# Attention output of two pairs of heads formed together in one full PSUM bank

## What is computed

```python
q = (xn @ Wq).reshape(b, n, h, dh).transpose(0, 2, 1, 3)      # 16 heads of 64
k, v = jnp.split(x @ Wkv, 2, axis=-1)                          # and two null keys and values for each head
q = _l2norm(q) * q_scale
k = _l2norm(k) * k_scale
sim = jnp.einsum('bhid,bhjd->bhij', q, k) * SCALE + slopes * bias   # causal, 258 keys
attn = jax.nn.softmax(sim, axis=-1)
out = jnp.einsum('bhij,bhjd->bhid', attn, v)
return out.transpose(0, 2, 1, 3).reshape(b, n, h * dh) @ Wout
```

## Time and profile before

| | |
|---|---|
| median of 3 runs | 492.96 us (492.75 to 495.38) |
| the profiled execution's own time | 497.05 us |
| its span, first to last instruction | 495.3 us |
| mean granted clock of TensorE | 0.956 of full speed |
| busy: TensorE, VectorE, ScalarE, GpSimd | 427.6, 372.1, 357.9, 322.0 us |

### The profile page before, as it was taken

One profiled execution on the slowest core, in us unless ns is written; L12 is line 12 of the kernel. 1 busy time (PEld: TensorE's weight loads), 2 busy tenths in 40 slices (PEclk: granted clock), 3 DMA queues, 4 the chain that ended last, 5 costly groups with the idle time before them and its releaser, 6 DMA issues.

```text
span 495.3 us, 10749 instructions
## 1 busy us (share of the span) xinstructions
PE 427.6 (86%) x2809; PEld 307.0 (62%) x2809; DVE 372.1 (75%) x1419; ACT 357.9 (72%) x1098; POOL 322.0 (65%) x492
## 2 busy tenths in 40 slices
PE   4846715999997998999999999999899999989985
PEld 3735413777775766767676666667566666767663
DVE  5698412656653996898799789889888988988884
ACT  3354512666666977988897897899789789878864
POOL 3748779700003789698877968877796897787150
PEclk9959765999999999999999999999999999999999
DMA  8961111222220000000001000000100000010010
GB/s 240 319 217 38 52 50 48 66 80 77 81 66 21 2 13 11 3 23 21 3 1 40 6 1 24 21 3 2 44 1 1 23 23 2 1 43 2 2 44 11
DMA packets 29739, 21.37 MB, mean 43 GB/s; under 512 B 3528, under 2 KB 27376, under 8 KB 29552
## 3 DMA queue, kind: packets, MB, share of 16 engines
q1 hardware_dynamic: 26816, 16.46, 11.2%
q0 software_dynamic: 2048, 4.20, 2.8%
q10 hardware_dynamic: 816, 0.03, 0.1%
HBM read 12.41 MB, written 8.26 MB: 42 GB/s over the span
## 4 chain that ended last, share of the span: by engine, by line
PE 34%; DVE 22%; POOL 18%; issue 11%; ACT 8%; another core or an unknown queue 4%; ACTq 1%; DMA 1%; DVEq 0%; POOLq 0%
PE bank L970 5%; POOL rnorm L425 5%; POOL arena_b L505 4%; DVE arena_b L899 4%; PE bank L972 4%; PE bank L1189 4%; PE bank L971 4%; PE bank L1119 4%; DVE arena_b L914 3%; DVE arena_b L876 3%; PE bank L1110 3%; POOL arena_b L441 2%; POOL rpow L428 2%; DVE probT L924 2%
## 5 line engine op out<-in xcount | busy, mean ns | idle before, releaser
L675 ACT ACTIVATE arena_b<-arena_b,nmx 128x130 f32<-128x130 f32 (+1 forms) x256 | 115.0, 458 | 30.6 <-DVE nmx L899 19.9
L899 DVE CUSTOM_DVE_ANT_0 arena_b<-bank,bias 128x130 f32<-128x130 f32 (+1 forms) x256 | 81.2, 355 | 24.0 <-PE bank L1119 19.0
L914 DVE TENSOR_SCALAR arena_b<-arena_b,rden 128x130 f32<-128x130 f32 (+1 forms) x256 | 82.6, 370 | 4.5
L428 POOL TENSOR_TENSOR rpow<-ssm,mhalf 128x8 f32<-128x8 f32 x32 | 53.0, 1655 | 34.1 <-DVE ssm L887 33.4
L1110 PE MATMUL bank<-ident,arena_b 128*128 128x128 f32 x384 | 67.0, 283 | 5.7 <-DVE arena_b L914 5.6
L441 POOL TENSOR_TENSOR arena_b<-arena_b,rnorm 128x512 f32<-128x512 f32 x64 | 68.1, 1065 | 5.0
L1119 PE MATMUL bank<-arena_a 64*128 64x130 f32 (+1 forms) x512 | 59.5, 351 | 0.8 <-ACT arena_a L636 0.8
L1110 PEld LDWEIGHTS bank<-ident,arena_b 128*128 128x128 f32 x384 | 43.8, 141 | 24.8 <-DVE arena_b L914 13.6
L883 DVE TENSOR_REDUCE ssq<-arena_b 128x8 f32<-128x512 f32 x64 | 43.6, 682 | 14.0 <-issue 13.3
L613 ACT ACTIVATE arena_b<-bank 128x512 f32<-128x512 f32 x64 | 38.1, 596 | 20.8 <-PE bank L972 9.7
L425 POOL TENSOR_TENSOR rnorm<-ssm,mhalf 128x8 f32<-128x8 f32 x32 | 52.8, 1650 | 0.0
(11 more groups left out here) (209 smaller groups left out, 1036.8 us busy)
## 6 DMA issues: line engine op xcount, KB each, us to landing
slot_x<-probT SPq DMA_DIRECT2D x3, 832.0 KB, 8.5
arena_b<-slot_x SPq DMA_DIRECT2D x39, 64.0 KB, 2.0
slot_y<-arena_b SPq DMA_DIRECT2D x39, 64.0 KB, 1.5
arena_a<-in_L_attn_x_dram SPq DMA_DIRECT2D x2, 512.0 KB, 5.2
arena_b<-in_L_ffn_wd_dram SPq DMA_DIRECT2D x1, 1024.0 KB, 9.8
arena_b<-in_L_attn_Wkv_dram SPq DMA_DIRECT2D x1, 1024.0 KB, 8.5
arena_b<-in_L_attn_x_dram SPq DMA_DIRECT2D x8, 128.0 KB, 2.3
out_dram<-arena_b SPq DMA_DIRECT2D x8, 128.0 KB, 1.9
```

What stands on the lines that cost most here:

```text
L428: gp.tensor_tensor(rpow[:, j, :], ssm[:, j, :], mhalf[:, 0:HEADS // 2], ALU.pow).then_inc(g.pw, 1)
L675: sc.activation(prob[:, h % 4, c], sim[h % 2][:, c], ACT.Exp, scale=-1.0, bias=nmx[:, h % HEADS, t:t + 1], accum_out=den[:, h % HEADS, t:t ...
L899: ve.tensor_tensor_reduce(out=sim[h % 2][:, c], in0=bank[h % 2][:, c], in1=bias[:, c], scale=-SLOPES[h], scalar=3e38, op0=ALU.add, op1=ALU ...
L914: ve.tensor_scalar(pr, pr, rden[:, h % HEADS, t:t + 1], None, ALU.mult).then_inc(g.pn, 1)
```

## The change

The output of two pairs of heads (four heads, "a four") is formed together in every fourth step, into the two halves of bank 4, and copied and counted once. The buffers of transposed probabilities become two for even and two for odd heads, used by pairs in turn, and oT gets twice the columns. The semaphores pvd, oev and oread count fours, and every wait on them is rewritten accordingly. With four f (heads 4f to 4f+3): the eight matmuls (sixteen instructions) come at step 4f+7 on TensorE, ScalarE's copy of 512 columns at step 4f+8, and two output projections at step 4f+9. Before, pair p had these at steps 2p+5, 2p+6 and 2p+7.

```diff
-        probT = [sb(f"probT{i}", [P, 3 * P]) for i in range(2)]
+        probT = [[sb(f"probT{half}_{i}", [P, 3 * P]) for i in range(2)] for half in range(2)]
-        oT = [sb(f"oT{i}", [P, SEQ]) for i in range(2)]
+        oT = [sb(f"oT{i}", [P, 2 * SEQ]) for i in range(2)]
-        opair = bank[4][:, 0:SEQ]
+        ofour = bank[4]
...
-                        act.wait_ge(g.pvd, PAIRS * b + PAIRS // 2)
+                        act.wait_ge(g.pvd, FOURS * b + FOURS // 2)
...
-                    if h is not None and h % 2:
-                        p = h // 2
-                        act.wait_ge(g.pvd, PAIRS * b + p + 1)
-                        if part != "first" or p >= 2:
-                            act.wait_ge(g.oread, PAIRS * b + p - 1)
-                        sc.activation(oT[p % 2][:], opair, ACT.Copy).then_inc(g.oev, 1)
+                    if h is not None and h % 4 == 3:
+                        f = h // 4
+                        act.wait_ge(g.pvd, FOURS * b + f + 1)
+                        if part != "first" or f >= 2:
+                            act.wait_ge(g.oread, FOURS * b + f - 1)
+                        sc.activation(oT[f % 2][:], ofour[:], ACT.Copy).then_inc(g.oev, 1)
...
-                        if part != "first" or h >= 2:
-                            dve.wait_ge(g.pvd, PAIRS * b + h // 2)
-                        ve.tensor_copy(probT[0][:], bank[2][:, 0:3 * P]).then_inc(g.ptev_d, 1)
+                        if part != "first" or h >= 4:
+                            dve.wait_ge(g.pvd, FOURS * b + h // 4)
+                        ve.tensor_copy(probT[0][h // 2 % 2][:], bank[2][:, 0:3 * P]).then_inc(g.ptev_d, 1)
...
-                    if h is not None and h % 2:
-                        p = h // 2
-                        if part != "first" or p >= 1:
-                            pe.wait_ge(g.oev, PAIRS * b + p)
-                        for half, evacuated in ((0, g.ptev_d), (1, g.ptev_a)):
-                            pe.wait_ge(evacuated, PAIRS * b + p + 1)
...
+                    if h is not None and h % 4 == 3:
+                        f = h // 4
+                        if part != "first" or f >= 1:
+                            pe.wait_ge(g.oev, FOURS * b + f)
+                        for p in (2 * f, 2 * f + 1):
+                            o = p % 2 * SEQ
+                            for half, evacuated in ((0, g.ptev_d), (1, g.ptev_a)):
+                                pe.wait_ge(evacuated, PAIRS * b + p + 1)
+                                r, hh, pT = slice(half * DH, (half + 1) * DH), 2 * (p % PAIRS) + half, probT[half][p % 2]
+                                te.matmul(ofour[r, o:o + SEQ], v[:, 0, hh * DH:(hh + 1) * DH], pT[:, 0:SEQ], start=True, stop=False)
+                                ins = te.matmul(ofour[r, o + P:o + SEQ], v[:, 1, hh * DH:(hh + 1) * DH], pT[:, SEQ:3 * P],
+                                                start=False, stop=True)
                         ins.then_inc(g.pvd, 1)
...
-                        te.matmul(bank[6][:, 0:SEQ], wo[:, p % PAIRS, :], oT[p % 2][:], start=p == 0,
-                                  stop=p == -1).then_inc(g.oread, 1)
+                        pe.wait_ge(g.oev, FOURS * b + f + 1)
+                        for p in (2 * f, 2 * f + 1):
+                            ins = te.matmul(bank[6][:, 0:SEQ], wo[:, p % PAIRS, :], oT[f % 2][:, p % 2 * SEQ:(p % 2 + 1) * SEQ],
+                                            start=p == 0, stop=p == -1)
+                        ins.then_inc(g.oread, 1)
```

More of the change, by code:

```diff
@@ L23 @@
 PAIRS = HEADS // 2
+FOURS = HEADS // 4
 K0 = NNULL + P
@@ L185, in build @@
         nk2, nv2 = sb("nk2", [32, 2, DH]), sb("nv2", [32, 2, DH])
-        nvT = probT[1][:, 0:PAIRS * 36]
-        zeros = probT[0][:, 0:DIM]
+        nvT = probT[1][0][:, 0:PAIRS * 36]
+        zeros = probT[0][0][:, 0:DIM]
         S = {n: sem(n) for n in [
@@ L632, in side_out @@
                     if c == 0 and part != "ready":
-                        act.wait_ge(g.pvd, PAIRS * b + PAIRS // 2)
+                        act.wait_ge(g.pvd, FOURS * b + FOURS // 2)
                     if c == 1 and part != "first":
-                        act.wait_ge(g.pvd, PAIRS * b)
+                        act.wait_ge(g.pvd, FOURS * b)
                     sc.activation(v[:, t, c * 512:(c + 1) * 512], side[i][:], ACT.Copy).then_inc(left[i], 1)
@@ L660, in entry @@
                         act.wait_ge(g.ptps, HEADS * b + h + 1)
-                        if part != "first" or h >= 2:
-                            act.wait_ge(g.pvd, PAIRS * b + h // 2)
-                        sc.activation(probT[1][:], bank[3][:, 0:3 * P], ACT.Copy).then_inc(g.ptev_a, 1)
+                        if part != "first" or h >= 4:
+                            act.wait_ge(g.pvd, FOURS * b + h // 4)
+                        sc.activation(probT[1][h // 2 % 2][:], bank[3][:, 0:3 * P], ACT.Copy).then_inc(g.ptev_a, 1)
                     if s == 6 and "prev" in whose:
-                        act.wait_ge(g.oread, PAIRS * b)
+                        act.wait_ge(g.oread, FOURS * b)
                         act.wait_ge(g.fin, b)
@@ L1127, in entry @@
                     h = head_at(part, s, 6)
-                    if h is not None and h % 2:
-                        p = h // 2
-                        if p == 0 and part != "first":
+                    if h is not None and h % 4 == 3:
+                        f = h // 4
+                        if f == 0 and part != "first":
                             pe.wait_ge(g.yev, b)
-                        pe.wait_ge(g.oev, PAIRS * b + p + 1)
-                        te.matmul(bank[6][:, 0:SEQ], wo[:, p % PAIRS, :], oT[p % 2][:], start=p == 0,
-                                  stop=p == -1).then_inc(g.oread, 1)
+                        pe.wait_ge(g.oev, FOURS * b + f + 1)
[3 more added lines that the diff above has]
+                        ins.then_inc(g.oread, 1)
                     if s == 13 and "own" in whose:
```

4 lines of the change are left out of this document (removed).

## The result

The changed kernel takes 498.3 us (median of 8 runs, 496.61 to 501.66) where the kernel before, run on the same chip beside it, takes 492.97 us (8 runs, 491.88 to 495.38). The ratio is 1.0105, 95% interval 1.0082 to 1.0128: slower by 1.05%, above my range of 489.5 to 497. The profiled execution took 498.89 us, its span 497.1 us.

The account below looks back on a forecast made before the run. No engine full, so the chain through GpSimd, TensorE, ScalarE and VectorE decides. Terms: -0.3 first element, +0.6 six periods, -0.5 and -0.3 last element, +1.05 tail = +0.55 on 492.96, so 493.5 us; range 489.5 to 497.

Parts of the forecast that it names:

- Start: ... the burst gone from step 1 gives nothing.: Start of each period, on TensorE: GpSimd's split releases it, so removing step 1's burst gains nothing.
- Step 1: a second projection, +0.44.: Step 1 of each period, on TensorE: a second output projection adds 0.44 us.
- step 5's missing burst: Step 5 on TensorE: burst gone, -0.90 us, of which 0.35 comes early because VectorE and ScalarE hold its successors.
- +0.1 a period: VectorE's start after step 6's scores: +0.1 us in each of six periods, +0.6; bounds -0.9 and +0.44.
- In the TensorE stretch from 445 us two bursts of two pairs stand for four of one: -0.5.: Start of the last element, 445 to 466 us, TensorE fully busy: fewer, merged bursts save 0.5 us.
- The merge, 0.25 each: TensorE's output bursts: each merge saves 0.25 us, 32 of them 8 us, counted only where the chain shows TensorE.
- The tail, +1.05: End of the last element: last burst of two pairs uncovered, longer copy, two projections; the end moves by +1.05 us.
- ScalarE's copy, -0.3 in the first element: First element, step 6: a copy that stood on the chain leaves, -0.3 us.
- The -0.3 in the last element: Last element, step 14: a ScalarE copy ahead of the probabilities' copy leaves the chain, -0.3 us.
- Waits and buffers at nothing: New waits on probT buffers and output bank: costed at nothing, covered by TensorE's program order.
- TensorE's time counts: Rival, faster: TensorE time counts wherever saved, 487.5 us, or 486 if all 32 merges count; chance 0.2.
- The double burst delays VectorE in step 7: Rival, slower: step 7's later transposes delay VectorE's copy, up to 0.65 us a period, 497.4 us; chance 0.18.

Follow-up runs that it names:

- e10: Changed kernel with step 1's two output projections ahead of its side jobs in elements 2 to 7 only, element 1 left as changed; ratio 1.0048.
- e6: Changed kernel with the whole last element in pairs and the first seven elements in fours; ratio 1.01 (1.0069 to 1.013).
- e9: Changed kernel with step 1's two output projections ahead of its side jobs in element 1 only; ratio 1.0077.
- e4: Changed kernel with step 1's two output projections moved ahead of that step's side jobs, where TensorE waits for GpSimd's split; ratio 1.004.
- e12: The kernel before again, nothing edited, for a second profile; ratio 1.0003.
- e7: Changed kernel with step 1's output projections ahead of its side jobs and the last two pairs of the whole program alone; ratio 1.0028.
- e11: Changed kernel with all heads in pairs, in the new buffers, and step 1's single projection ahead of its side jobs; ratio 1.0005.
- e1: Changed kernel with pairs formed, copied and projected as before, in the new buffers and bank halves; ratio 1.0006.
- e2: Changed kernel with the last two pairs of each element alone and the other six in fours; ratio 1.0061.
- e8: Changed kernel with eight unread transposes in each of steps 1, 5, 9 and 13, which lost their bursts; ratio 1.011.
- e3: Changed kernel with eight unread transposes in step 1 of elements 1 to 6, ahead of the wait for the split; ratio 1.0111.

## Why the prediction was wrong

I had +0.55 us; it was +5.2 (4.0 to 6.3). By its steps:

- **"Start: ... the burst gone from step 1 gives nothing."** This step failed. I read that GpSimd's split releases TensorE there and concluded that the burst in the gap was worth nothing. It was worth nothing as time; but it was the work that kept the wait at 0.68 to 0.81 us. Without it TensorE stands 1.94 us in element 1 and 1.5 in the others, and in element 1 the clock goes to 0.50 for 3.4 us in three of four profiles (the changed kernel's two and e10's, not e6's). I had taken the clock at 1.00 as a given of the head loop. Measured: 1.7 us in the profile (e9, e6), 1.0 to 1.4 in the runs.
- **"Step 1: a second projection, +0.44."** The size is right (4.12 against 3.68 us). What failed is what I set against it: step 5's missing burst, with 0.35 that comes early, so that +0.1 a period was left. A period without a fall is 43.01 us in the changed kernel. The first profile of before has 42.95 from its element 2 on, and against that my +0.1 looks right; the second has 42.67 throughout, which makes it +0.34, near my upper bound of 0.44. With the projections put into the wait 0.25 of this goes in e10, 0.1 in e4. So the value depends on which profile one reads, and I had only the slower one of before.
- **"In the TensorE stretch from 445 us two bursts of two pairs stand for four of one: -0.5."** This was wrong in sign. A stretch with TensorE busy 21.00 of 21.00 isn't one in which only TensorE counts: ScalarE's copies were just in time for it. With step 1 late and the burst gone a wait of 0.93 us opened. The last stretch without its tail grew by 1.1 us (81.7 - 10.8 against 79.4 - 9.6), where I had -0.8 with ScalarE's copy, and e10 takes all of this 1.1 back.
- **The merge, 0.25 each.** The size was right: the page has 9.1 us less of TensorE's work for 32 of them (8.2 against e12's 426.7), and the burst of two pairs takes 1.50 us (329.64 to 331.14, below) against 2 x 0.80, which with the 0.10 ahead of a burst is 0.20 for a merge. I took it as worth nothing where GpSimd and VectorE carry the chain, and that held (e7 equals e11). What it saved wasn't on the chain. The rule of the Trainium skill that I named ahead (TensorEngine Tiling (Array Packing), Tiling Modes, Key Properties), that a change of the tiling mode drains TensorE, is in line with the 1.50 us. The burst, changed kernel:

```profile
329.64 0.66 PE L1103 MATMUL bank<-probT,arena_a 128*64 128x256 f32 x4
330.12 0.39 PE L1104 MATMUL bank<-probT,arena_a 128*64 128x128 f32 x4
330.34 0.65 PE L1103 MATMUL bank<-probT,arena_a 128*64 128x256 f32 x4
330.77 0.44 PE L1104 MATMUL bank<-probT,arena_a 128*64 128x128 f32 x4
331.14 0.55 PE L1113 MATMUL bank<-ident,arena_b 128*128 128x128 f32 x3
```

- **The tail, +1.05.** Right, 1.2 measured; every kernel with the last pairs alone has the old 9.6 or 9.7 (e1, e2, e6, e7, e11). Why e8 has 10.2, with fours to the end, is open.
- **ScalarE's copy, -0.3 in the first element.** Not seen: its period is 41.7 us in both kernels. The -0.3 in the last element isn't seen either, in a stretch that grew.
- **Waits and buffers at nothing.** Right (e1).
- **The rivals.** "TensorE's time counts" is false: e7 with 31 merges and e11 with none have the same stretches, and the 21 us that e8 puts onto TensorE cost no more than what the fall that it removes had cost. "The double burst delays VectorE in step 7" had the right side and nearly the right size (497.4 us), by luck: its reason didn't happen. VectorE's copy there follows its own instruction without a wait (changed kernel):

```profile
342.00 0.38 DVE L888 TENSOR_SCALAR ssm<-ssq 128x8 f32<-128x8 f32 x1
342.29 0.54 DVE L925 COPY probT<-bank 128x384 f32<-128x384 f32 x1
```

The 5.9 us of the profiles divide into 1.7 for the clock, 2.3 for the two output projections behind the wait of step 1 (0.2 in element 1, 1.0 in the four periods behind it, 1.1 in the last stretch), and 1.2 for the tail. That leaves 0.7 us, about what e7, with all three mended, has over the kernel before (0.5). The division is that of these profiles: the 1.0 lies within the spread between two profiles of one kernel, and the 1.7 stands only where the fall comes. Still open: how many of the runs without a profile have the fall (e9 gains 1.0 to 1.4 us in them and not 1.9; e6 shows that it can stay away), what makes it come or not, why e6's runs are no faster than the change, why the last stretch of e8 is as long as it is, and the 1 us by which e7's runs lie above e11's though their profiles are alike. No version of these beats the kernel before.

## What to carry to other kernels

Work that fills a wait of TensorE isn't free to take away: ask how long the engine then stands, and whether the clock holds over that gap in more than one profile, before writing "gives nothing". When instructions are regrouped, put those whose input is ready ahead of the instruction that waits; here that one move was worth more than half of the loss (1.0040 against 1.0105). An engine that is busy 100% of a stretch can still have no claim on saved time, if the next engine's results come just in time.

## What the runs showed of the hardware

- The granted clock fell to 0.50 for about 3.4 us after stretches in which TensorE wasn't wholly idle: 0.13 us of work in 2.00 (changed kernel), 0.43 in 2.00 and 2.38 in 4.00 (e3), 0.58 in 2.00 (e6). With 0.93 in 2.00 (e9) it held, and with 0.15 in 2.00 it held too (e6, element 1). Waits of 1.47 to 1.51 us in the other periods of the changed kernel brought no fall.
- The same wait in the same place brings a fall in one execution and none in another: 1.94 us in step 1 of element 1 with a fall in both profiles of the changed kernel and in e10, 1.93 without one in e6; 1.66 us at 389 to 390 us with one in e6, 1.65 without one in the changed kernel. None of the four profiles of kernels with pairs everywhere, whose wait for the split is 0.81 us at most, has a fall in the head loop.
- What a fall costs depends on where it comes: 1.7 us in step 1 of element 1, 1.9 at 397 us (e3), 0.3 at 391 us (e6).
- The kernel before has two lengths of period with the same instructions: 42.73 us, and 42.95 from element 2 on, in one profile, 42.67 throughout in the other. TensorE's wait for the split is 0.80 us in the short ones and 0.68 in the long ones of these two profiles; e1, with 42.74, has 0.67 or none. What makes it go one way or the other no run here shows.
